# Decoder layer on one core: unnormalised attention turned behind the second product, normalised attention in the next slot, splits ahead of the root, PE's waits for stacks a slot ahead

## Chip, core and metric

One core of a Trainium2 chip. The metric is the device time of one execution in microseconds (us); lower is better. Engines are named as in the profile: PE (matmuls; PEld its weight loads), DVE, ACT, POOL, and SP, which here only issues DMAs.

## What is computed

A post-norm decoder layer without causal mask over 32 sequences of 128 tokens and width 128, in float32: self-attention, cross-attention to a context, and a feed-forward part with fake-quantised integers, each followed by a residual and a layer norm.

```python
x = _layernorm(x + attn(x, wq, wk, wv, bq, bk, bv, wo, bo))      # 16 heads of 8
x = _layernorm(x + xattn(ctx, x, ctx, Wk, Wq, Wv, Wo))           # 16 heads of 8, no bias
x = _layernorm(x + ffn(x, W1, b1, W2, b2))                       # per-tensor int8 grids, exact gelu
```

## The kernel before

**Tasks and slots.** The attention part is 64 tasks, each one sequence of self (S) or cross (C) attention; tasks come in pairs (two sequences), 32 pairs in the order S0 to S5, then C0, S6, C1, S7 and so on to C9, S15, then C10 to C15. `over_slots` runs `slot(k)` for k from -5 to 67 on every engine, so the order of all instructions is written out by hand, engine by engine, and engines meet only in semaphores. In slot k PE works on several tasks at once: the first scores of task k+2 (called b in the code), the second scores of k and k-1 (a, z), the product with v of k-1 (z), and the closing steps of k-2 (w), k-3 (x) and k-6 (v).

**Two passes of scores.** Keys and queries are split into float16 parts and laid out by DMA in "stacks" (`arena_h`), four heads side by side, so that a matmul with few rows gives a head's scores. The first pass (L1083) goes into two PSUM banks, 1024 columns per half task, and DVE takes the row maximum over 128 keys of each of 8 heads (`neg_max`, L850). The maximum is turned by PE (L1156), copied and scaled by ACT (L657) and sent by DMA into a row of the stack, so that the second pass (L1090) gives shifted scores, from which ACT makes the exponentials (L652 and L663). Both passes are interleaved in `scores(half)`; a half can start when DVE has finished the maximum of the half before (semaphore `max_done`, in the code `mx`) and ACT its exponentials (`ex`).

**Closing steps of a task.** `product(half)` (L1109) gives unnormalised attention and the sums; ACT copies it (L673), PE turns it in two pieces (L1167, semaphore `tu`), DVE takes the reciprocal of the sums (L860) and multiplies (L869), PE turns the result (L1199, `ta`), ACT copies it (`attT`, L680), PE multiplies with the output weights (L1191, `oo`), DVE adds the residual (L890), takes statistics (L829) and mean and variance (L833, semaphore `ag`), POOL makes the root (`var_eps` L528 and `rstd` L531), and DVE writes the new x (L841, `xn`).

**The way of a stack.** The projection of a pair (PE L1124, L1131, L1144) is copied by ACT (L619, L646, L690) to `q_full`, `k_full`, `cq_full`, `ck_full`. POOL splits it in two instructions (helper `split`, L364 and L366), and SP sends it with three DMAs (`fill`, L399) of 64 KB. For a pair whose first task has place p, POOL splits sq or ck in slot p-5 and sk or cq in slot p-4; SP fills in the order sq, sk or ck, cq in its slot p-4. PE needs both stacks in `scores(0)` of slot p-2, which is an even slot. POOL's work in a slot is in this order: the root of a task, the split of sk or cq, `x_bias` (L549), the context values (L560), the split of sq or ck. Within a queue everything waits for what stands before it.

**After the attention** come the feed-forward stages (from 275 us in the profile), which the change does not touch.

Of the kernel before, what the change touches and what calls it, by code (L numbers as in the profile page):

```python
# [25 lines left out]
NTERM = 3  # L26
# [136 lines left out]
def decoder_layer(nc, xT, xN, cT, cN, wq, wk, wv, bq, bk, bv, woT_u, bo, Wk, Wq, Wv, woT_x,  # L163
                  w1T, b1, w2T, b2, out):
    with ExitStack() as ctx:
# [303 lines left out]
        def _(pool):  # L469
# [54 lines left out]
            def slot(k):  # L524
                for v in outputs(k):

                    pool.wait_ge(ag, v.pos + 1)
                    pool.tensor_tensor(var_eps[v.par][:, :], mean_var[v.place][:, 1:2], eps_col[:, :], ALU.add).then_inc(ve, 1)  # L528
                    pool.wait_ge(ve, v.pos + 1)
                    need(pool, xn, v.pos - 3)  # L530
                    pool.tensor_tensor(rstd[v.place][:, :], var_eps[v.par][:, :], minus_half[:, :], ALU.pow).then_inc(rq, 1)  # L531
# [5 lines left out]
                if i is not None:  # L537

                    pool.wait_ge(txe, 2 * i + 2)
                    split(pool, "cq", cq_full[i % RING][:, :], i)  # L540
                i = S_FIRST.get(k + BIAS_AT)
# [63 lines left out]
        def _(act):  # L605
# [4 lines left out]
            def slot(k):  # L610
                a, z, w, v, nxt = task(k), task(k - 1), task(k - 2), task(k - 6), task(k + 1)
# [41 lines left out]
                if nxt is not None:  # L653
# [20 lines left out]
                if w is not None:  # L674

                    act.wait_ge(ta, w.pos + 1)
                    if v is not None and v.kind == "S":
                        act.wait_ge(tx, v.m + 1)
                    need(act, oo, w.pos)
                    act.copy(attT[:, :], ps_x[:, 0:S]).then_inc(tae, 1)  # L680
# [81 lines left out]
        def _(dve):  # L762
# [61 lines left out]
            def slot(k):  # L824
# [32 lines left out]
                if w is not None:  # L857
                    u = ps_t[:, 0:2 * S].rearrange("p (h c) -> p h c", c=16)
                    dve.wait_ge(tu, w.pos + 1)
                    dve.reciprocal(r_sum[:, :], u[:, :, E]).then_inc(rs, 1)  # L860
# [5 lines left out]
                if w is not None:  # L866
                    dve.wait_ge(rs, w.pos + 1)
                    need(dve, ta, w.pos)
                    dve.tensor_tensor(att[:, :, :], u[:, :, 0:E], r_sum[:, :].unsqueeze(2).broadcast_to([128, H, E]),  # L869
                                      ALU.mult).then_inc(an, 1)  # L870
                if k == 1:
                    folded_weights()
                if k == 2:
                    weight_top()
# [3 lines left out]
                if k == 2:  # L878
                    weight_scale()
                    own_step(dve.reciprocal(w_inv[:, :], w_scale[:, :]))  # L880
# [10 lines left out]
                if k <= LATE_STATS:  # L891
                    for t in outputs(k):
                        new_x(t)
                if late is not None:
                    mean_variance(late)
# [140 lines left out]
        def _(pe):  # L1036
# [19 lines left out]
            def slot(k):  # L1056
# [7 lines left out]
                def scores(half):  # L1064

                    s, s_half = (z, 1) if half == 0 else (a, 0)
                    if b is not None:
                        if half == 0 and b.half == 0:
                            for n in (b.q, b.k):
                                pe.wait_ge(s_stack[n][b.ring], landed(b.pair, RING, 16 * NTERM))  # L1070
                        need(pe, mx, 2 * b.pos + half)
                    if s is not None:
                        if s_half == 0:
                            pe.wait_ge(s_maxrow[s.par], 16 * (s.pos // 2 + 1))
                        need(pe, ex, 2 * s.pos + s_half)
                    for j in range(HQ):
                        for g in range(GROUPS_HALF):
# [9 lines left out]
                            if s is not None:  # L1087
# [4 lines left out]
                                if last:  # L1092
                                    ins.then_inc(p2, 1)

# [224 lines left out]
```

## Time and profile before

| | |
|---|---|
| median of 3 runs | 356.62 us (354.52 to 357.43) |
| profiled execution, its own time | 355.31 us |
| its span in the profile | 353.5 us |
| busy of the span: PE, DVE, ACT, POOL | 265.0, 314.0, 252.5, 187.0 us |
| attention part | to 274 us |
| granted TensorE clock, mean | 0.916 of full speed |

The profile is of one execution. Around its span lie 1.8 us that the profile does not see. Slots of the attention part can be told apart by DVE's `neg_max` instructions, two per slot.

### The profile page before, as it was taken

How to read it: one execution, taken by the hardware profiler on the slowest of the kernel's cores; microseconds unless marked ns; L12 is line 12 of the kernel's file. 1: busy time of each engine (PE TensorE's matmuls, PEld its weight loads, DVE VectorE, ACT ScalarE, POOL GpSimd, SP SyncE). 2: the span in 40 equal slices, each digit the busy share in tenths (PEclk: the TensorE clock that was granted, in tenths of full speed). 3: DMA queues.
4: the chain of work that ended last, by engine and by line, in shares of the span. 5: the costliest groups of instructions: out<-in, count | busy, mean ns of one | idle time of the engine just before them, and what ended most of it. 6: DMA issues, size and time to landing. Idle time of an engine off the chain costs nothing.

```text
span 353.5 us, 13237 instructions
## 1 busy us (share of the span) xinstructions
PE 265.0 (75%) x4897; PEld 171.0 (48%) x4899; DVE 314.0 (89%) x720; ACT 252.5 (71%) x502; POOL 187.0 (53%) x382
## 2 busy tenths in 40 slices
PE   3678887989989999999899988898883365102980
PEld 2446564656656666666665655555551122001660
DVE  5756799989999999999999999999889599997894
ACT  2135877988889888888888887887762599605855
POOL 6234869656675666657675667665222006400275
PEclk9999999999999999999999999999995578755797
DMA  1352323233332332323323242332000000000034
GB/s 52 89 159 69 99 80 88 63 108 90 97 107 74 107 104 84 101 84 102 106 83 107 79 124 84 96 94 71 5 3 0 0 0 0 0 0 3 1 90 149
DMA packets 48998, 25.19 MB, mean 71 GB/s; under 512 B 6440, under 2 KB 48808, under 8 KB 48936
## 3 DMA queue, kind: packets, MB, share of 16 engines
q1 hardware_dynamic: 46936, 23.76, 23.4%
q8 instruction: 41, 0.67, 0.8%
q10 hardware_dynamic: 2000, 0.59, 0.7%
q14 instruction: 21, 0.17, 0.2%
HBM read 9.39 MB, written 2.10 MB: 32 GB/s over the span
## 4 chain that ended last, share of the span: by engine, by line
DVE 32%; PE 30%; POOL 14%; issue 13%; DMA 4%; ACT 3%; SPq 2%; ACTq 0%; POOLq 0%; DVEq 0%; another core or an unknown queue 0%
DVE neg_max L850 14%; PE ps L1083 8%; PE ps L1109 7%; DVE h_ext L957 5%; DVE h_ext L958 5%; DMA arena_h<-parts_sk 4%; POOL rstd L531 3%; PE ps L1167 2%; PE ps L1156 2%; SPq L399 2%; PE ps L1124 2%; PE ps L1144 2%; PE ps L1131 2%; PE ps L1251 1%; POOL o_root L598 1%
## 5 line engine op out<-in xcount | busy, mean ns | idle before, releaser
L850 DVE TENSOR_REDUCE neg_max<-ps 128x8 f32<-128x1024 f32 x128 | 157.2, 1228 | 18.5 <-PE ps L1083 16.0
L652 ACT ACTIVATE probs<-ps 128x1024 f32<-128x1024 f32 x64 | 65.6, 1025 | 19.7 <-PE ps L1090 18.2
L1083 PE MATMUL ps<-arena_h 31*128 31x128 f16 x1024 | 52.8, 221 | 27.3 <-DVE neg_max L850 17.9
L663 ACT ACTIVATE probs<-ps 128x1024 f32<-128x1024 f32 x64 | 65.7, 1026 | 8.5 <-PE ps L1090 8.5
L1083 PEld LDWEIGHTS ps<-arena_h 31*128 31x128 f16 x1024 | 31.0, 94 | 59.9 <-DVE neg_max L850 35.6
L1090 PE MATMUL ps<-arena_h 32*128 32x128 f16 x1024 | 51.7, 219 | 0.6 <-ACT probs L652 0.5
L528 POOL TENSOR_TENSOR var_eps<-mean_var,eps_col 128x1 f32<-128x1 f32 x64 | 12.2, 191 | 73.4 <-DVE mean_var L833 73.4
L1109 PE MATMUL ps<-probs,arena_q 128*32 128x128 f32 x1024 | 42.1, 283 | 0.9 <-issue 0.9
L1109 PE MATMUL ps<-probs,arena_h 128*32 128x128 f32 x1024 | 41.6, 281 | 0.2 <-ACT probs L652 0.2
L531 POOL TENSOR_TENSOR rstd<-var_eps,minus_half 128x1 f32<-128x1 f32 x64 | 35.2, 550 | 5.0
L1090 PEld LDWEIGHTS ps<-arena_h 32*128 32x128 f16 x1024 | 29.6, 93 | 1.6 <-ACT probs L663 0.5
L1109 PEld LDWEIGHTS ps<-probs,arena_q 128*32 128x32 f32 x1024 | 24.5, 110 | 7.8 <-issue 1.4
L1109 PEld LDWEIGHTS ps<-probs,arena_h 128*32 128x32 f32 x1024 | 24.2, 109 | 6.9 <-ACT probs L652 0.4
L1167 PE MATMUL ps<-ident,u_sb 128*128 128x128 f32 x128 | 24.8, 276 | 0.0
L673 ACT COPY u_sb<-ps 128x256 f32<-128x256 f32 x64 | 23.6, 369 | 1.1 <-PE ps L1109 1.1
L957 DVE TENSOR_REDUCE h_ext<-arena_h 128x1 f32<-128x1024 f32 (+1 forms) x17 | 19.5, 1148 | 3.2 <-ACT arena_h L711 3.2
L680 ACT COPY attT<-ps 128x128 f32<-128x128 f32 x64 | 17.6, 276 | 5.6 <-PE ps L1199 5.5
L581 POOL TENSOR_TENSOR x_all<-x_all,b_wide 128x1024 f32<-128x1024 f32 x4 | 9.3, 2354 | 22.1 <-DVE x_int L952 22.1
L1199 PE MATMUL ps<-ident,att 128*128 128x128 f32 x64 | 18.0, 281 | 3.3 <-DVE att L869 3.2
L958 DVE TENSOR_REDUCE h_ext<-arena_h 128x1 f32<-128x1024 f32 (+1 forms) x17 | 19.5, 1146 | 0.0
L364 POOL TENSOR_TENSOR parts_sq<-q_full,zero_col 128x256 f16<-128x256 f32 x15 | 9.2, 612 | 18.2 <-ACT q_full L619 18.2
L711 ACT ACTIVATE arena_h<-ps,b_sb,quant 128x1024 f32<-128x1024 f32 (+1 forms) x17 | 18.6, 1194 | 0.3 <-remote 0.3
(155 smaller groups left out, 626.4 us busy)
## 6 DMA issues: line engine op xcount, KB each, us to landing
arena_h<-parts_sq SPq DMA_DIRECT2D x48, 64.0 KB, 2.0
arena_h<-parts_ck SPq DMA_DIRECT2D x48, 64.0 KB, 2.1
arena_h<-parts_cq SPq DMA_DIRECT2D x48, 64.0 KB, 2.0
arena_h<-parts_sk SPq DMA_DIRECT2D x45, 64.0 KB, 2.0
xT_in<-in_xT_dram SPq DMA_DIRECT2D x16, 128.0 KB, 2.6
xN_in<-in_xN_dram SPq DMA_DIRECT2D x16, 128.0 KB, 2.7
cT_in<-in_cT_dram SPq DMA_DIRECT2D x16, 128.0 KB, 2.4
cN_in<-in_cN_dram SPq DMA_DIRECT2D x16, 128.0 KB, 2.6
```

What stands on the lines that cost most here:

```text
L531: pool.tensor_tensor(rstd[v.place][:, :], var_eps[v.par][:, :], minus_half[:, :], ALU.pow).then_inc(rq, 1)
L652: act.activation(probs[1][:, :], ps_s2, ACT.Exp, scale=SCALE).then_inc(ex, 1)
L663: act.activation(probs[0][:, :], ps_s2, ACT.Exp, scale=SCALE).then_inc(ex, 1)
L673: act.copy(u_sb[:, :], ps_u[:, 0:2 * S]).then_inc(ue, 1)
L711: act.activation(hT[:, hc, tok], src, ACT.Gelu, bias=b1_sb[:, hc:hc + 1], scale=qs[0][:, OUT:OUT + 1]).then_inc(f_g, 1)
L850: dve.tensor_reduce(neg_max[b.par][:, HH * half:HH * half + HH], ps_s1.rearrange("p (h k) -> p h k", h=HH), AXX, ALU.max, negate=True).the ...
L957: dve.tensor_reduce(h_ext[:, 0, col:col + 1], h, AXX, ALU.max).then_inc(f_mx, 1)
L958: dve.tensor_reduce(h_ext[:, 1, col:col + 1], h, AXX, ALU.min, negate=True).then_inc(f_mx, 1)
L1083: ins = pe.matmul(ps_s1[:, at:at + S], q[r:r + MAX_AT, j, :], kk[r:r + MAX_AT, j, :], start=True, stop=True, skip_group_check=True)
L1090: ins = pe.matmul(ps_s2[:, at:at + S], kk[r:r + GROUP_ROWS, j, :], q[r:r + GROUP_ROWS, j, :], start=True, stop=True, skip_group_check=True)
L1109: last = pe.matmul(ps_u[32 * j:32 * j + 32, half * S:(half + 1) * S], heads_of[:, HQ * (GROUPS_HALF * half + g) + j, :], probs[half][:, (H ...
L1167: last = pe.transpose(ps_t[:, blk * S:(blk + 1) * S], u_sb[:, blk * S:(blk + 1) * S], ident[:, :])
```

## The change

The changes by engine:

The diff is in the order of the file: `roots`, then POOL, ACT and PE (whose helpers `scores` and `stacks` come first); DVE's part is left out.

- PE: the two transposes of `u_sb` stand behind `product(1)` and not behind `product(0)`. The transpose of `att` is made a slot later, behind `product(0)`, ahead of that of the maximum. The waits for a pair's stacks stand in a helper `stacks()` at the end of the slot before, ahead of the output product. In `scores` the wait for the maximum is written last.
- ACT: the copy `attT` stands in the next slot, between the scaled maximum and the copies of projections, and not at the slot's end.
- DVE: between the two maxima of a slot stand statistics, new x, and mean and variance; between the second and the next slot's first stand reciprocal, residual sum and multiplication.
- POOL: the splits of sk and cq stand ahead of the root, and the root is that of task k-4 and not of k-5 (helper `roots`).

```diff
+def roots(k):
+
+    if k <= LATE_STATS:
+        return [task(k - 4)] if task(k - 4) is not None else []
+    return [t for t in outputs(k) if t.pos > LATE_STATS - 4]
...
-                for v in outputs(k):
-
-                    pool.wait_ge(ag, v.pos + 1)
...
                 i = S_FIRST.get(k + FILL_AT)
                 if i:
                     pool.wait_ge(eqk, 2 * i + 2)
                     split(pool, "sk", k_full[:, :], i)
...
                     split(pool, "cq", cq_full[i % RING][:, :], i)
+                for v in roots(k):
+
+                    pool.wait_ge(ag, v.pos + 1)
...
+                if x is not None:
+                    act.wait_ge(ta, x.pos + 1)
+                    need(act, oo, x.pos)
+                    act.copy(attT[:, :], ps_x[:, 0:S]).then_inc(tae, 1)
                 if k >= LEAD_SLOTS:
                     evacuations()
...
-                    if b is not None:
-                        if half == 0 and b.half == 0:
-                            for n in (b.q, b.k):
-                                pe.wait_ge(s_stack[n][b.ring], landed(b.pair, RING, 16 * NTERM))
-                        need(pe, mx, 2 * b.pos + half)
                     if s is not None:
                         if s_half == 0:
                             pe.wait_ge(s_maxrow[s.par], 16 * (s.pos // 2 + 1))
                         need(pe, ex, 2 * s.pos + s_half)
+                    if b is not None:
+                        need(pe, mx, 2 * b.pos + half)
...
+                def stacks():
+
+                    t = task(k + 3)
+                    if t is not None and t.half == 0:
+                        for n in (t.q, t.k):
+                            pe.wait_ge(s_stack[n][t.ring], landed(t.pair, RING, 16 * NTERM))
...
                 scores(0)
                 product(0)
+                if x is not None:
+                    pe.wait_ge(an, x.pos + 1)
...
+                    pe.transpose(ps_x[:, 0:S], att[:, :, :].rearrange("p h e -> p (h e)"), ident[:, :]).then_inc(ta, 1)
...
                     pe.transpose(ps_x[0:H, S:2 * S], neg_max[nxt.par][:, :], ident[:, :]).then_inc(mt, 1)
+
+                if k >= LEAD_SLOTS:
+                    projections()
+
+                scores(1)
+                product(1)
...
                 if w is not None:
                     pe.wait_ge(ue, w.pos + 1)
                     need(pe, an, w.pos)
...
                     for blk in range(2):
                         last = pe.transpose(ps_t[:, blk * S:(blk + 1) * S], u_sb[:, blk * S:(blk + 1) * S], ident[:, :])
                     last.then_inc(tu, 1)
-
-                if k >= LEAD_SLOTS:
-                    projections()
-
-                scores(1)
-                product(1)
...
+                stacks()
                 if x is not None:
                     pe.wait_ge(tae, x.pos + 1)
...
                     pe.matmul(ps_o[:, 0:D], attT[:, :], (wo_self if x.kind == "S" else wo_cross)[:, :],
                               start=True, stop=True, skip_group_check=True).then_inc(oo, 1)
-                if w is not None:
-
-                    pe.wait_ge(an, w.pos + 1)
...
-                    pe.transpose(ps_x[:, 0:S], att[:, :, :].rearrange("p h e -> p (h e)"), ident[:, :]).then_inc(ta, 1)
```

PE at the end of slot 21, with the start of slot 22, before. In square brackets are the semaphores that PE waits for ahead of the instruction: the last-named is a wait of the instruction itself, those before it stand in wait instructions of their own, one or two in each.

```order
L1191 MATMUL ps<-wo_self,attT 128x128 [waits qk_full_out,y_done,attT_out]
L1199 MATMUL ps<-ident,att 128x128 [waits attT_out,cq_full_out,max_rows_out,att_done]
L1208 MATMUL ps<-ident,arena_q 128x128 [waits x_new_done]
L1083 MATMUL ps<-arena_h 128x128 [waits max_done,exp_done,stack_ck3_landed,stack_cq3_landed]
L1090 MATMUL ps<-arena_h 128x128
```

The same place now, from the turned u on:

```order
L1196 MATMUL ps<-ident,u_sb 128x128 [waits att_done,u_out]
L1196 MATMUL ps<-ident,u_sb 128x128
L1211 MATMUL ps<-wo_self,attT 128x128 [waits y_done,attT_out,qk_full_out,stack_ck3_landed,stack_cq3_landed]
L1218 MATMUL ps<-ident,arena_q 128x128 [waits attT_out,max_rows_out,x_new_done]
L1084 MATMUL ps<-arena_h 128x128 [waits max_done,exp_done]
L1091 MATMUL ps<-arena_h 128x128
```

The stacks' waits moved from the scores to the output product, and `max_done` still stands in a wait instruction ahead of the scores' first matmul. In the second half of slot 21, and in the first half of an odd slot, it stood on the matmul itself. Before:

```order
L1131 MATMUL ps<-xT_in1,wk_g 128x256 [waits qk_full_out,y_done]
L1083 MATMUL ps<-arena_h 128x128 [waits exp_done,max_row_landed1,max_done]
```

and now:

```order
L1162 MATMUL ps<-ident,att 128x128 [waits attT_out,cq_full_out,max_rows_out,att_done]
L1175 MATMUL ps<-ident,neg_max0 16x128 [waits attT_out,max_rows_out,cq_full_out,max_done,masks_ready]
L1139 MATMUL ps<-xT_in1,wk_g 128x256 [waits qk_full_out,y_done]
L1084 MATMUL ps<-arena_h 128x128 [waits max_done,exp_done,max_row_landed1]
```

So `max_done` went from the matmul to a wait instruction ahead of it. POOL from slot 24 (split of cq, pair C4) to slot 26 (split of sk, pair S10), before:

```order
L364 TENSOR_TENSOR parts_cq<-cq_full0,zero_col 128x256
L366 TENSOR_TENSOR parts_cq<-cq_full0,parts_cq 128x256
L528 TENSOR_TENSOR var_eps0<-mean_var0,eps_col 128x1
L531 TENSOR_TENSOR rstd0<-var_eps0,minus_half 128x1
L560 TENSOR_TENSOR arena_h<-cN_in0,zero_col 128x4x4x8 x2
L364 TENSOR_TENSOR parts_sq<-q_full,zero_col 128x256
L366 TENSOR_TENSOR parts_sq<-q_full,parts_sq 128x256
L528 TENSOR_TENSOR var_eps1<-mean_var1,eps_col 128x1
L531 TENSOR_TENSOR rstd1<-var_eps1,minus_half 128x1
L364 TENSOR_TENSOR parts_sk<-k_full,zero_col 128x256
L366 TENSOR_TENSOR parts_sk<-k_full,parts_sk 128x256
```

and now:

```order
L371 TENSOR_TENSOR parts_cq<-cq_full0,zero_col 128x256
L373 TENSOR_TENSOR parts_cq<-cq_full0,parts_cq 128x256
L544 TENSOR_TENSOR var_eps0<-mean_var0,eps_col 128x1
L547 TENSOR_TENSOR rstd0<-var_eps0,minus_half 128x1
L544 TENSOR_TENSOR var_eps1<-mean_var1,eps_col 128x1
L547 TENSOR_TENSOR rstd1<-var_eps1,minus_half 128x1
L567 TENSOR_TENSOR arena_h<-cN_in0,zero_col 128x4x4x8 x2
L371 TENSOR_TENSOR parts_sq<-q_full,zero_col 128x256
L373 TENSOR_TENSOR parts_sq<-q_full,parts_sq 128x256
L371 TENSOR_TENSOR parts_sk<-k_full,zero_col 128x256
L373 TENSOR_TENSOR parts_sk<-k_full,parts_sk 128x256
```

Two roots now stand together ahead of the context values and the split of sq; the split of sk follows that of sq at once. The second of the two (`mean_var1`) is that of slot 25's own mean and variance.

## Rows read from the trace of the kernel before

**Rows 1.** Busy time by engine in one stretch: from:to, length, PE, PEld, DVE, ACT, POOL.

```profile
62.00:206.00 144.00, 132.59 (x2906) 88.83 (x2894) 137.97 (x317) 123.55 (x272) 93.49 (x191) 1.00 0.33 94
```

**Rows 2.** The chain that ended last: start, length, what, from 125 us.

```profile
125.32 0.24 issue
...
129.03 0.04 issue
```

**Rows 3.** Timeline of DVE, end of slot 24 to the start of 26.

```profile
120.59 1.23 DVE L850 TENSOR_REDUCE neg_max<-ps 128x8 f32<-128x1024 f32 x1
...
122.32 1.23 DVE L850 TENSOR_REDUCE neg_max<-ps 128x8 f32<-128x1024 f32 x1
123.46 0.25 DVE L860 RECIPROCAL r_sum<-ps 128x16 f32<-128x16 f32 x1
123.63 0.23 DVE L829 BATCH_NORM_STATS2 stats<-y_sb 128x6 f32<-128x128 f32 x1
...
124.09 1.23 DVE L850 TENSOR_REDUCE neg_max<-ps 128x8 f32<-128x1024 f32 x1
125.23 0.28 DVE L890 TENSOR_TENSOR y_sb<-ps,x_bias 128x128 f32<-128x128 f32 x1
125.43 0.34 DVE L841 TENSOR_SCALAR x_all<-y_sb,mean_var,rstd 128x128 f32<-128x128 f32 x1
125.68 0.17 DVE L833 BATCH_NORM_AGGREGATE mean_var<-stats 128x2 f32<-128x6 f32 x1
126.01 1.23 DVE L850 TENSOR_REDUCE neg_max<-ps 128x8 f32<-128x1024 f32 x1 [0.15 <-PE ps L1083]
```

**Rows 4.** Timeline of DVE and PE at the two shared extremes.

```profile
273.94 0.17 DVE L943 TENSOR_REDUCE ext<-x_ext 128x2 f32<-128x18 f32 x1
...
274.17 0.37 PE L1224 MATMUL ps<-ident,ext 128*2 128x128 f32 x1 [3.54 <-DVE ext L943]
...
319.62 0.19 DVE L973 TENSOR_REDUCE ext<-h_ext 128x2 f32<-128x34 f32 x1
...
319.95 0.37 PE L1224 MATMUL ps<-ident,ext 128*2 128x128 f32 x1 [18.01 <-DVE ext L973]
```

**Rows 5.** Timeline of POOL, slots 25 and 26.

```profile
122.44 0.19 POOL L528 TENSOR_TENSOR var_eps<-mean_var,eps_col 128x1 f32<-128x1 f32 x1 [1.55 <-DVE mean_var L833]
...
123.22 0.76 POOL L560 TENSOR_TENSOR arena_h<-cN_in,zero_col 128x128 f32<-128x128 f32 x2
123.94 0.61 POOL L364 TENSOR_TENSOR parts_sq<-q_full,zero_col 128x256 f16<-128x256 f32 x1
...
126.72 0.61 POOL L364 TENSOR_TENSOR parts_sk<-k_full,zero_col 128x256 f16<-128x256 f32 x1
```

**Rows 6.** Timeline of SP at pair S10, and landings of all sk fills from 62 us.

```profile
125.37 2.38 SPq L399 DMA_DIRECT2D arena_h<-parts_sq  x3
128.11 1.92 SPq L399 DMA_DIRECT2D arena_h<-parts_sk  x3
...
DMA to landing us min/median/max: 1.9/2.1/3.5
```

**Rows 7.** First and last of 25 fills: chain and timeline at S6 and C15.

```profile
71.31 3.48 DMA arena_h<-parts_sk
...
72.53 1.23 DVE L850 TENSOR_REDUCE neg_max<-ps 128x8 f32<-128x1024 f32 x1
...
243.11 2.26 SPq L399 DMA_DIRECT2D arena_h<-parts_cq  x3
...
246.19 1.23 DVE L850 TENSOR_REDUCE neg_max<-ps 128x8 f32<-128x1024 f32 x1
```

**Rows 8.** Timeline of DVE and POOL at 66.5 us.

```profile
66.67 0.63 DVE L841 TENSOR_SCALAR arena_q<-y_sb,mean_var,rstd 128x128 f32<-128x128 f32 x1
...
66.55 0.67 POOL L366 TENSOR_TENSOR parts_sq<-q_full,parts_sq 128x256 f16<-128x256 f32 x1
```

**Rows 9.** Timeline of ACT in slot 25.

```profile
123.75 0.47 ACT L619 ACTIVATE k_full<-ps,bqk_sb 128x256 f32<-128x256 f32 x1 [0.22 <-PE ps L1131]
```

More of the change, by code:

```diff
@@ L540, in slot @@
                     split(pool, "cq", cq_full[i % RING][:, :], i)
+                for v in roots(k):
+                    pool.wait_ge(ag, v.pos + 1)
+                    pool.tensor_tensor(var_eps[v.par][:, :], mean_var[v.place][:, 1:2], eps_col[:, :], ALU.add).then_inc(ve, 1)
+                    pool.wait_ge(ve, v.pos + 1)
+                    need(pool, xn, v.pos - 3)
+                    pool.tensor_tensor(rstd[v.place][:, :], var_eps[v.par][:, :], minus_half[:, :], ALU.pow).then_inc(rq, 1)
                 i = S_FIRST.get(k + BIAS_AT)
@@ L673, in slot @@
                     act.copy(u_sb[:, :], ps_u[:, 0:2 * S]).then_inc(ue, 1)
-                if w is not None:
[L676 to L680, printed above, removed]
                 if k == 3:
@@ L865, in slot @@
                         new_x(t)
[L866 to L870, printed above, removed]
+                if k <= LATE_STATS:
+                    for t in outputs(k):
+                        new_x(t)
+                if late is not None:
+                    mean_variance(late)
                 if k == 1:
                     folded_weights()
-                if k == 2:
-                    weight_top()
+                if k == 3:
+                    weight_scale()
+                    own_step(dve.reciprocal(w_inv[:, :], w_scale[:, :]))
                 maximum(1)
@@ L877, in slot @@
                     weight_extremes()
-                if k == 2:
-                    weight_scale()
-                    own_step(dve.reciprocal(w_inv[:, :], w_scale[:, :]))
+                if w is not None:
+                    u = ps_t[:, 0:2 * S].rearrange("p (h c) -> p h c", c=16)
+                    dve.wait_ge(tu, w.pos + 1)
+                    dve.reciprocal(r_sum[:, :], u[:, :, E]).then_inc(rs, 1)
                 if x is not None:
@@ L890, in slot @@
                     dve.tensor_tensor(dst, own, residual, ALU.add).then_inc(yy, 1)
[L891 to L895, printed above, removed]
+                if w is not None:
+                    dve.wait_ge(rs, w.pos + 1)
+                    need(dve, ta, w.pos)
+                    dve.tensor_tensor(att[:, :, :], u[:, :, 0:E], r_sum[:, :].unsqueeze(2).broadcast_to([128, H, E]),
+                                      ALU.mult).then_inc(an, 1)
+                if k == 2:
+                    weight_top()
                 if k >= LATE_STATS and x is not None:
@@ L1148, in slot @@
                 product(0)
+                if x is not None:
+                    pe.wait_ge(an, x.pos + 1)
+                    need(pe, mte, tasks_to(k))
+                    need(pe, tae, x.pos)
+                    need(pe, txe, s_to(k - 7))
+                    pe.transpose(ps_x[:, 0:S], att[:, :, :].rearrange("p h e -> p (h e)"), ident[:, :]).then_inc(ta, 1)
+                    if x.pos == 0:
+                        pe.wait_ge(w_diag, 1)
+                        pe.matmul(ps_t[:, 3 * S:3 * S + 2], ones_2[:, :], w_top_diag[:, :], start=True, stop=True,
+                                  skip_group_check=True).then_inc(w_shared, 1)
                 if nxt is not None:
@@ L1192, in slot @@
                               start=True, stop=True, skip_group_check=True).then_inc(oo, 1)
[L1193 to L1195 removed]
+                if v is not None and v.kind == "S":
+                    pe.wait_ge(xn, v.pos + 1)
                     need(pe, mte, tasks_to(k + 1))
                     need(pe, tae, tasks_to(k - 3))
[L1198 to L1207 removed]
                     pe.transpose(ps_x[:, 2 * S:3 * S], x1_all[:, v.m, :], ident[:, :]).then_inc(tx, 1)
```

28 lines of the change are left out of this document (6 added, 22 removed).

## The prediction, as it was made

> **What bounds the kernel now.** I read, in this order, the busy times by stage, the chain that ended last, the timelines of DVE, POOL and SP over slots 24 to 28, and the rows where something is late. The stage from 62 to 206 us is DVE's: 137.97 busy of 144.00 us [rows 1]. The chain goes from `neg_max` to PE's scores and back, twice a slot. A half slot is 1.23 us of maximum and a gap in which PE makes the next half's scores: in slot 25 the first maximum ends at 123.55 and the second starts at 124.09 (gap 0.54); that one ends at 125.32 and slot 26's first starts at 126.01 (gap 0.69) [rows 3]. Ahead of odd slot 25 the gap is 0.50 (120.59 + 1.23 to 122.32) [rows 3]. The 0.19 more comes ahead of every even slot, where PE also waits for two stacks: the chain has 0.24 us of "issue" at 125.32 and 0.04 at 129.03 [rows 2]. DVE's small instructions fit in these gaps and start at distances of 0.15 to 0.25 us [rows 3].
>
> **A wait instruction that stands behind a late semaphore.** The built program puts `max_done`, in the even case, in the first of two wait instructions ahead of the matmul, in the odd case on the matmul itself; so two instructions are run after the maximum, for 0.19 us. A second pair of rows gives the price of one: L1224 starts 0.06 us after DVE's L943 where it waits for it itself (273.94 + 0.17 to 274.17), and 0.14 us after L973, for which a wait instruction stands ahead (319.62 + 0.19 to 319.95) [rows 4]. So 0.08 to 0.10 us each.
>
> **Part 1, order of the waits.** The change takes the stacks' waits out of the scores, but writes `max_done` last, and the built order then puts it in a wait instruction ahead of the matmul in all halves. Gap now: 0.50 + 0.08 = 0.58, I take 0.59 for each. A pair of slots has four gaps: before 0.69 + 0.55 + 0.50 + 0.54 = 2.28; now 4 x 0.59 = 2.36. The gap of 0.54 before the second half was PE's own work (a projection stands there), and the change takes one transpose of two from it; that gain goes under the 0.59. Over 27 pairs of slots: +2 us, between 0 (0.57) and +4 (0.61). The gain that one would read from the diff, 27 x 0.19 = 5 us, is given back three times over one half each.
>
> The Trainium skill says the same of waits ("Perfetto Trace Analysis", Identifying Dependency Chains): an instruction that waits for several engines may get EventSemaphore instructions ahead of it. It gives no price; by the rule alone the sum would have the stacks' waits cheaper by one place and nothing on the other halves. The sum above goes by rows 2 to 4.
>
> **Part 2, PE, ACT and DVE.** The turns of u and att only change places: PE loses 0.11 us between product(0) and scores(1) and gains it behind product(1), where it waits for DVE anyway. ACT's copy of `attT` goes where ACT idles 0.22 us for a projection [rows 9]: nothing, since the next exponentials wait for PE's scores; at worst 0.1 us a slot, if the copies reach past them. On DVE the gap within a slot now holds statistics, new x and mean: 0.16 + 0.25 + 0.2, the other reciprocal, residual and multiplication: 0.17 + 0.20 + 0.2 (distances in rows 3); both begin 0.09 us before the maximum ends, so both fit in 0.59. Tail and early slots: the same work, 0, within 1 us.
>
> **Part 3, the splits, which decides.** Before, POOL in slot 25 waited for mean and variance from the end of slot 24 (var_eps at 122.44), then context values at 123.22, split of sq at 123.94; the sk split starts at 126.72 and ends at 128.08 [rows 5]. Now the root in slot 25 is that of slot 25's own statistics. DVE's mean ends at about the first maximum's start + 1.74 = 124.06. So var_eps starts at 124.14, +0.78 root, +0.72 values: the split of sq starts at 125.64, 1.7 us later than before. The split of sk follows at once and is ready at 128.36, only 0.3 later, for it no longer has a root ahead. But SP is one queue: sq's three DMAs start at 127.08 (before 125.37), take 1.92 as those of sk did, and sk's start at 129.00 (before 128.11), 0.9 us later [rows 6]. The same sum for cross pairs (the ck split is held, x_bias takes the place of the values) gives cq 0.83 later.
>
> What margin is there? Before, the third DMA of sk for S10 starts near 129.4 and lands 1.9 later, 131.3, and PE needs it when the second maximum of slot 27 ends, at 132.5: 1.2 us. Now 0.9 is lost and 0.12 won by longer slots: 0.4. And the wait stands earlier. Behind it on PE are the output product and the turn of x1; DVE's residual sum waits for that product, and the next maximum stands behind the sum. From a landing to that maximum I count 0.14 (a wait instruction and start) + 0.49 (product) + 0.05 + 0.20 + 0.20 = 1.1 us, against a normal 0.59 after the maximum's end; so a fill is late when its margin is under 0.5. Undisturbed fills then cost 0.1 us each.
>
> Most aren't undisturbed: sk's DMAs land in 1.9 to 3.5 us, median 2.1 [rows 6]. The same subtraction over the 25 fills from S6 (71.31 + 3.48 = 74.79 against a maximum's end of 72.53 + 1.23 = 73.76: -1.03) to C15 (all three issued by 243.11 + 2.26 = 245.4, the last landed at 246.7, against 246.19 + 1.23 = 247.42: +0.7) [rows 7] gives a mean of 0.57. Moved by 0.75 and needed 0.49 earlier, that lacks 0.67 us a fill, 17 us in all if each paid by itself. It doesn't: a fill's way spans 2.5 slots, so when one pair stalls, the next has that much more time. Taking each stall off the next lack, in order, leaves 11 us; 1.2 of it is paid before (S6, S8). So +10 us. Bounds: +4 (the fills are 0.5 us less late than I count), +20 (two fills back to back issue and land slower, as S6 did).
>
> The Trainium skill's advice for DMAs ("DMA: Bandwidth & Descriptors", Rules for kernel authors) is to issue early and to wait late. The change does the reverse in both; rows 5 to 7 put its price here.
>
> **Part 4, new x beside a split.** New x took 0.63 in place of 0.34 us at 66.67, and ended 0.08 after the POOL split at 66.55 to 67.22 [rows 8]: it reads and writes SBUF only, and waits for POOL. In the new place it stands 1.30 after a slot's start; in even slots POOL then has the first instruction of a split, to about 1.66, and if DVE gets in between the two, it ends at 1.74, ahead of the maximum at 1.82: 0. If it doesn't, 0.6 us for each of 27 slots, 16 us. I take 0 to 4, +1, since the two instructions of a split are 0.08 us apart. The skill ("GPSIMD Engine Reference", Key points) names this sharing of the SBUF interfaces; it has no time for it.
>
> **Sum.** 355.3 (own time of the profiled execution) + 2 + 10 + 1 = 368. The median of the runs shown is 1.3 above that execution, well within the error of the 10. An effect under 1% (3.6 us) can't be told from none.
>
> **Rivals.**
> 1. *The stacks are in time, only the waits' order counts.* For it: on a calm fill the margin of 0.4 misses 0.5 by 0.1, and the longer slots give more. Against: the spread of landings. Time: 355.3 + 2 = 357. Chance 0.13.
> 2. *Faster: the wait instructions cost nothing once they are ahead.* The price at the scores comes only from two of them in a row, a single one is hidden under PE's weight load, and the stacks are in time; this decides from the point where less than 0.04 us of the 0.08 is seen. Then all gaps are 0.50: 27 x (2.28 - 2.00) = 7.6, and the stalls of S6 and S8 go: 347 to 349. For it: sk's own split is no longer behind a root, and the diff gathers all waits away from the scores. Against: rows 4 show a single one at 0.08, and SP's queue order. Chance 0.09.
> 3. *Contention decides*: new x waits for both parts of a split in each even slot, stalls of the stacks are partly covered by it: 355.3 + 2 + 16 + 4 = 377. Chance 0.15.
> 4. My forecast, about 368 (360 to 374): 0.63.
>
> **How the numbers follow.** Slower by over 1%: 0.63 + 0.15 = 0.78; within 1%: 0.13; faster: 0.09. The range reaches from rival 1 to rival 3: 355 to 379.
>
> **What would show it.** PE's L1084 waiting for DMAs of sk and cq, or, since the wait moved, PE's output product L1211 doing so, in more than 10 places and over 8 us in total; POOL's sq split starting 3.3 us after a slot's first maximum instead of 1.6; calm gaps between maxima of 0.58 to 0.60 in all four places; no "issue" of 0.24. Wrong if the gaps are 0.50 (then a single wait instruction is free), or if fills land more than 1 us before use. Rival 3 shows in new x rows over 0.5 us that end with a POOL split.

## The result, and the profile after

The changed kernel takes 373.9 us (median of 4 runs, 370.2 to 376.5), the kernel before beside it 355.8 us (4 runs): 1.050 times as long, interval 1.044 to 1.056. Its profiled execution took 373.43 us, with a span of 371.7. The span before was 353.5, so 18.2 us are to be explained.

**Where the 18.2 us lie.** I cut both traces at DVE's maxima (L850 before, L854 now):

| stretch | before | after | difference |
|---|---|---|---|
| start of the span to slot 9's first maximum | 63.6 | 67.5 | +4.0 |
| from there to slot 61's second maximum | 189.7 | 205.0 | +15.2 |
| from there to the end | 100.2 | 99.2 | -1.0 |

The middle stretch holds 53 slots, and the maxima themselves take the same in both (129.8 and 129.5 us). The rest of it are the gaps ahead of them, in sum:

| gap ahead of | before | after |
|---|---|---|
| an even slot's first maximum | 19.4 | 28.0 |
| its second | 14.1 | 17.3 |
| an odd slot's first | 13.6 | 15.9 |
| its second | 14.6 | 15.9 |

Busy times by engine, for the stretch of [rows 1]: DVE is busy for 129.05 us instead of 137.97, so it waits more. The granted clock of TensorE, third from the end, is 0.99 instead of 1.00.

```profile
62.00:206.00 144.00, 128.46 (x2671) 84.52 (x2670) 129.05 (x292) 116.66 (x251) 87.09 (x179) 0.99 0.31 88
```

DVE's timeline of the calm slot 25, which answers to [rows 3]:

```profile
129.74 0.27 DVE L896 TENSOR_TENSOR att<-ps,r_sum 128x128 f32<-128x128 f32 x1
130.10 1.23 DVE L854 TENSOR_REDUCE neg_max<-ps 128x8 f32<-128x1024 f32 x1
131.24 0.28 DVE L833 BATCH_NORM_STATS2 stats<-y_sb 128x6 f32<-128x128 f32 x1
131.44 0.33 DVE L845 TENSOR_SCALAR x_all<-y_sb,mean_var,rstd 128x128 f32<-128x128 f32 x1
131.69 0.18 DVE L837 BATCH_NORM_AGGREGATE mean_var<-stats 128x2 f32<-128x6 f32 x1
131.91 1.22 DVE L854 TENSOR_REDUCE neg_max<-ps 128x8 f32<-128x1024 f32 x1
...
133.73 1.23 DVE L854 TENSOR_REDUCE neg_max<-ps 128x8 f32<-128x1024 f32 x1
```

Here the gaps are 131.91 - 131.33 = 0.58 and 133.73 - 133.13 = 0.60, where they were 0.54 and 0.69. DVE's small instructions end 0.04 to 0.09 us ahead of the next maximum (131.69 + 0.18 against 131.91), so they fit, as costed.

POOL's timeline for the same slot, and the start of the next; it answers to [rows 5]:

```profile
131.94 0.19 POOL L544 TENSOR_TENSOR var_eps<-mean_var,eps_col 128x1 f32<-128x1 f32 x1 [2.64 <-DVE mean_var L837]
132.21 0.55 POOL L547 TENSOR_TENSOR rstd<-var_eps,minus_half 128x1 f32<-128x1 f32 x1
132.72 0.76 POOL L567 TENSOR_TENSOR arena_h<-cN_in,zero_col 128x128 f32<-128x128 f32 x2
133.44 0.61 POOL L371 TENSOR_TENSOR parts_sq<-q_full,zero_col 128x256 f16<-128x256 f32 x1
134.13 0.67 POOL L373 TENSOR_TENSOR parts_sq<-q_full,parts_sq 128x256 f16<-128x256 f32 x1
134.76 0.61 POOL L371 TENSOR_TENSOR parts_sk<-k_full,zero_col 128x256 f16<-128x256 f32 x1
135.45 0.67 POOL L373 TENSOR_TENSOR parts_sk<-k_full,parts_sk 128x256 f16<-128x256 f32 x1
```

The root waits 2.64 us for a mean that ends in the middle of the slot, and only then come values, split of sq, split of sk. The split of sq starts 3.34 us after the slot's first maximum (133.44 - 130.10). SP then sends what POOL has left behind. The rows answer to [rows 6]. The last one is for the five DMAs that SP issued from 135.4 to 138.1 us; the longest of them, 2.9, is the third of sk, issued at 138.09:

```profile
134.87 1.82 SPq L406 DMA_DIRECT2D arena_h<-parts_sq  x3
136.74 1.95 SPq L406 DMA_DIRECT2D arena_h<-parts_sk  x3
...
DMA to landing us min/median/max: 1.9/2.4/2.9
```

So the stack is there at 141.0, while the last maximum that needs nothing of it ends at 140.39. DVE and PE at that place, the end of slot 27:

```profile
139.17 1.22 DVE L854 TENSOR_REDUCE neg_max<-ps 128x8 f32<-128x1024 f32 x1
140.31 0.25 DVE L882 RECIPROCAL r_sum<-ps 128x16 f32<-128x16 f32 x1
141.60 0.29 DVE L892 TENSOR_TENSOR y_sb<-ps,arena_q 128x128 f32<-128x128 f32 x1 [1.04 <-PE ps L1211]
...
142.01 1.21 DVE L854 TENSOR_REDUCE neg_max<-ps 128x8 f32<-128x1024 f32 x1
```

```profile
141.10 0.46 PE L1211 MATMUL ps<-wo_cross,attT 128*128 128x128 f32 x2 [1.03 <-issue]
```

The gap is 1.62 instead of 0.59 us. Note what the last row gives as the cause: "issue". The wait for the stack is in a wait instruction of its own ahead of the matmul, and the profile doesn't always trace such a wait to its DMA. The list of waits of the whole kernel after therefore has them under three names:

```profile
POOL var_eps L544 <- DVE mean_var L837: 95.8, 48, 3.7
DVE y_sb L892 <- PE ps L1211: 14.5, 13, 2.4
PEld ps L1211 <- issue: 13.4, 10, 2.8
...
PEld ps L1211 <- DMA arena_h<-parts_cq: 4.4, 6, 1.8
```

The second row is the one that counts, for DVE sets the pace: 13 times the residual sum waited for an output product, 14.5 us in all; before, it did so once, for 1.0 us. The first row was 73.4 us in 62 places before.

The page's chain, which had "DVE 32%; PE 30%; POOL 14%" of the span before, now runs through POOL:

```profile
POOL 36%; issue 33%; DVE 17%; PE 9%; ACT 2%; DMA 1%; POOLq 0%; ACTq 0%; DVEq 0%; another core or an unknown queue 0%
```

Read such an "issue" with the timeline beside it. A piece of it on this chain goes from 136.90 to 139.16; the first row of the list of waits says what POOL waited for there: the mean of the next slot. It is a wait for DVE, and no cost of issuing.

**The early part**, slots 2 to 8. PE's product of 16 matmuls, after:

```profile
34.84 1.08 PE L1117 MATMUL ps<-probs,arena_q 128*32 128x128 f32 x16 [0.69 <-issue]
37.57 1.08 PE L1117 MATMUL ps<-probs,arena_q 128*32 128x128 f32 x16
39.68 0.64 PE L1117 MATMUL ps<-probs,arena_q 128*32 128x128 f32 x16 [0.22 <-issue]
```

and before:

```profile
30.44 1.08 PE L1109 MATMUL ps<-probs,arena_q 128*32 128x128 f32 x16
33.82 0.65 PE L1109 MATMUL ps<-probs,arena_q 128*32 128x128 f32 x16 [0.90 <-issue]
```

The same 16 matmuls took 1.08 us until 38.6 us after, and until 31.5 before. The step lies where the trace's first record of the granted clock begins, at 38.7 us after and at 31.5 before, with 1.00 (2.4 GHz) in both; the 1.00 that the profile prints for earlier times only says that there is no record. In slot 8 the record falls to 0.50 (1.2 GHz) from 62.6 to 66.0 us after, and the 16 matmuls take 1.08 us again; before, it stays at 1.00. So up to 38.7 us the matmuls ran at the pace of the lower clock. The lines are the product in slot 8 and the stretch around it, as from:to, length, PE, granted clock, share and GB/s of the DMAs, first after and then before:

```profile
62.58 1.08 PE L1117 MATMUL ps<-probs,arena_q 128*32 128x128 f32 x16
62.00:66.00 4.00, 4.00 (x63) 0.58 0.37 108
```

```profile
62.00:66.00 4.00, 3.89 (x90) 1.00 0.29 85
```

Ahead of this fall PE waited: it was busy for 1.42 of the 4 us from 58 to 62, since the stacks of S5 landed at 61.7 instead of 59.5. Slot 2's gaps were 2.34 and 2.27 us where they had been 1.17 and 1.80, and slot 8's 2.97 and 1.81 instead of 2.44 and 0.56. The changed kernel is 2.35 us behind at slot 3's first maximum (40.09 against 37.74), 2.65 at slot 8's and 4.0 at slot 9's; so nearly all of the 4.0 us arises in the two stretches in which its matmuls take the time of the lower clock and those of the kernel before don't.

In `a_order` and `a_root5` the profiled execution was a disturbed one with a lower granted clock, so of these two profiles only gaps and waits are read, and of the four runs of `a_order` only one, 365.5 us, was undisturbed (the others took 373.3 to 379.5).

### The profile page after: what moved, and what is told of

Same layout as the page of the kernel before. It is cut to its first block, busy times and chain, and to the rows that moved or that the text cites. A ratio compares the mean times of both kernels' runs of the same rounds, so it can differ in the third digit from the quotient of the medians.

```text
span 371.7 us, 13270 instructions
## 1 busy us (share of the span) xinstructions
PE 276.9 (75%) x4897; PEld 177.0 (48%) x4899; DVE 315.7 (85%) x720; ACT 257.1 (69%) x502; POOL 185.4 (50%) x382
## 4 chain that ended last, share of the span: by engine, by line
POOL 36%; issue 33%; DVE 17%; PE 9%; ACT 2%; DMA 1%; POOLq 0%; ACTq 0%; DVEq 0%; another core or an unknown queue 0%
POOL rstd L547 7%; DVE h_ext L961 5%; DVE h_ext L962 4%; POOL var_eps L544 3%; POOL arena_h L567 3%; POOL parts_ck L373 3%; POOL x_bias L556 3%; POOL parts_cq L371 3%; POOL parts_ck L371 2%; POOL parts_cq L373 2%; POOL parts_sq L373 2%; POOL parts_sq L371 2%; POOL parts_sk L371 2%; DVE neg_max L854 2%; PE ps L1084 1%
## 5 line engine op out<-in xcount | busy, mean ns | idle before, releaser
L854 DVE TENSOR_REDUCE neg_max<-ps 128x8 f32<-128x1024 f32 x128 | 156.4, 1222 | 21.4 <-PE ps L1084 16.0
L659 ACT ACTIVATE probs<-ps 128x1024 f32<-128x1024 f32 x64 | 65.5, 1024 | 30.1 <-PE ps L1091 29.0
L674 ACT ACTIVATE probs<-ps 128x1024 f32<-128x1024 f32 x64 | 65.5, 1024 | 9.1 <-PE ps L1091 7.0
L1084 PE MATMUL ps<-arena_h 31*128 31x128 f16 x1024 | 54.1, 224 | 19.2 <-DVE neg_max L854 11.6
L1084 PEld LDWEIGHTS ps<-arena_h 31*128 31x128 f16 x1024 | 33.7, 95 | 52.3 <-issue 31.8
L1091 PE MATMUL ps<-arena_h 32*128 32x128 f16 x1024 | 52.8, 222 | 0.6 <-ACT probs L659 0.6
L1117 PE MATMUL ps<-probs,arena_q 128*32 128x128 f32 x1024 | 43.6, 291 | 0.9 <-issue 0.9
L1117 PEld LDWEIGHTS ps<-probs,arena_q 128*32 128x32 f32 x1024 | 25.4, 114 | 8.2 <-issue 2.1
L1196 PE MATMUL ps<-ident,u_sb 128*128 128x128 f32 x128 | 28.2, 302 | 0.0
L1162 PE MATMUL ps<-ident,att 128*128 128x128 f32 x64 | 21.6, 338 | 4.2 <-DVE att L896 4.2
L1211 PE MATMUL ps<-wo_cross,attT 128*128 128x128 f32 x64 | 14.2, 305 | 8.2 <-issue 7.3
L668 ACT COPY attT<-ps 128x128 f32<-128x128 f32 x64 | 15.3, 239 | 5.8 <-PE ps L1162 5.8
L1196 PEld LDWEIGHTS ps<-ident,u_sb 128*128 128x128 f32 x128 | 13.2, 143 | 12.3 <-issue 12.3
```

Source lines behind the costliest of these rows:

```text
L659: act.activation(probs[1][:, :], ps_s2, ACT.Exp, scale=SCALE).then_inc(ex, 1)
L674: act.activation(probs[0][:, :], ps_s2, ACT.Exp, scale=SCALE).then_inc(ex, 1)
L854: dve.tensor_reduce(neg_max[b.par][:, HH * half:HH * half + HH], ps_s1.rearrange("p (h k) -> p h k", h=HH), AXX, ALU.max, negate=True).the ...
L1084: ins = pe.matmul(ps_s1[:, at:at + S], q[r:r + MAX_AT, j, :], kk[r:r + MAX_AT, j, :], start=True, stop=True, skip_group_check=True)
L1091: ins = pe.matmul(ps_s2[:, at:at + S], kk[r:r + GROUP_ROWS, j, :], q[r:r + GROUP_ROWS, j, :], start=True, stop=True, skip_group_check=True)
L1117: last = pe.matmul(ps_u[32 * j:32 * j + 32, half * S:(half + 1) * S], heads_of[:, HQ * (GROUPS_HALF * half + g) + j, :], probs[half][:, (H ...
```

## The experiments

Names with a_ are the changed kernel with one or more parts taken back, those with b_ the kernel before with one part added. Ratios are to the kernel before in the same session (medians 354.1, 354.1 and 353.7 us). "Stage" is the middle stretch of the first table: 189.7 us before, 205.0 after.

### `a_roots`: the root at the slot's start again

```diff
             def slot(k):
+                for v in outputs(k):
+                    pool.wait_ge(ag, v.pos + 1)
...
-                for v in roots(k):
-                    pool.wait_ge(ag, v.pos + 1)
```

> The changed kernel, but POOL makes the root where it made it before: at the start of its slot, of task k-5, ahead of all splits. Its mean and variance are then half a slot old, so POOL need not wait. Theory 'POOL's wait in mid slot makes sq and ck late': the split of sq starts 1.6 us earlier against the slot or more, the stalls of over 1 us in even slots mostly go, calm gaps stay 0.59: 373.9 - 12 = 360 to 364. Rival 'the stacks are late because PE waits for them ahead of the output product': stays within 3 us of 374.

Measured: 356.9 us, ratio 1.009 (1.005 to 1.013); stage 193.0; calm gaps 0.59 in all four places. Gaps that exceed the calm one by more than 0.1 us, called stalls from here on, are four, 2.4 us above it in sum; the changed kernel has 17, with 14.4 us. POOL and SP, slots 25 and 26:

```profile
121.30 0.19 POOL L535 TENSOR_TENSOR var_eps<-mean_var,eps_col 128x1 f32<-128x1 f32 x1 [0.25 <-DVE mean_var L837]
...
122.79 0.61 POOL L371 TENSOR_TENSOR parts_sq<-q_full,zero_col 128x256 f16<-128x256 f32 x1
...
125.65 0.61 POOL L371 TENSOR_TENSOR parts_sk<-k_full,zero_col 128x256 f16<-128x256 f32 x1
```

```profile
124.23 2.73 SPq L406 DMA_DIRECT2D arena_h<-parts_sq  x3
127.04 1.85 SPq L406 DMA_DIRECT2D arena_h<-parts_sk  x3
```

With slot 25's first maximum at 121.21, the split of sq starts 1.58 us after it, as before, and the first DMA of sk 5.8 us after it instead of 6.6. Of the 5.0% that the change costs, 4.1 go with this one part. The time is below the 360 to 364 us that I expected, since the early part came back too (slot 9 at 63.3 us, with the full clock from 29.5 us on).

### `a_root5`: the root behind the split, but an older task's

```diff
-                for v in roots(k):
+                for v in outputs(k):
```

> The changed kernel, but the root that stands behind the splits of sk and cq is that of task k-5, as before the change, whose mean and variance are half a slot old; nothing else differs. Theory 'what makes the fills late is that POOL waits for the middle of DVE's slot': the loss of the late fills goes as in a_roots, 355 to 360. Rival 'it is the place behind the split that matters': stays at 370 or more.

Measured: 362.4 us, ratio 1.021 (1.015 to 1.027). The stalls ahead of even slots are gone (1.1 us in two places, calm gap 0.59), and no output product waits for a DMA. So it is whose root stands there that makes the stacks late, not that a split stands ahead of it. The place has a price of its own, and that I had too low: in even slots the gap ahead of the second maximum is 0.81 us, since new x now waits for a root that begins behind a split.

```profile
POOL var_eps L544 <- DVE mean_var L837: 45.5, 36, 3.7
...
DVE arena_q L845 <- POOL rstd L547: 7.5, 14, 2.3
```

### `a_stacks`: the stacks' waits behind the output product

```diff
-                stacks()
                 if x is not None:
                     pe.wait_ge(tae, x.pos + 1)
...
                     pe.matmul(ps_o[:, 0:D], attT[:, :], ...).then_inc(oo, 1)
+                stacks()
```

> The changed kernel, but stacks() stands behind the output product and not ahead of it, so that no instruction that DVE waits for stands behind the stacks' waits. Theory: a late fill then costs 0.5 us less in each of some 12 places: 366 to 371. Rival 'only the place of that wait is at fault': 357 to 361, since before the change the fills were in time for the scores.

Measured: 368.7 us, ratio 1.042 (1.034 to 1.049); stalls 10.2 us in 14 places instead of 14.4 in 17; stage 200.7. DVE's residual sum no longer waits for a late stack, and the stalls are 4.3 us less. The interval overlaps that of the changed kernel, but the stage, 4.3 us shorter, says the same as the stalls. It is the smaller part.

### `a_order` and `b_last`: the order of the waits

`a_order` writes the maximum's wait first again in the changed kernel; `b_last` writes it last in the kernel before, and changes nothing else.

```diff
-                        need(pe, mx, 2 * b.pos + half)
                     if s is not None:
...
                         need(pe, ex, 2 * s.pos + s_half)
+                    if b is not None:
+                        need(pe, mx, 2 * b.pos + half)
```

> The changed kernel, but in scores() the wait for the maximum is written first again, so that the build puts it on the matmul itself and the exponentials' wait ahead of it. If a wait instruction behind the late semaphore costs 0.09 us, calm gaps between maxima fall from 0.59 to 0.50. Theory 'late stacks decide': slots get 0.36 us a pair shorter, but the fills' way from POOL's root to landing stays as long, so the stalls grow by nearly as much: time 367 to 373, 0 to 6 us below the changed kernel. Rival 'the order of the waits is the whole loss': back to 352 to 358.

> The kernel before with one edit: in scores() the wait for the maximum is written last, so that the build puts it in a wait instruction ahead of the matmul in every half; the stacks' waits stay in the scores. Theory (0.09 us for a wait instruction behind the late semaphore): gaps 0.69, 0.59, 0.59, 0.59 in place of 0.69, 0.55, 0.50, 0.54, that is 0.18 us in each of 27 pairs of slots, +4 to +5 us, 1.3% slower than before. Rival 'the calm gap of 0.59 in the changed kernel comes from DVE's new order': gaps stay, same as before.

Measured, `b_last`: 357.6 us, ratio 1.011 (1.006 to 1.015), stage 192.5. All four gaps are 0.59, while I had expected 0.69 to stay ahead of even slots. DVE's maxima in it, at a distance of 1.82 us throughout:

```profile
119.87 1.23 DVE L850 TENSOR_REDUCE neg_max<-ps 128x8 f32<-128x1024 f32 x1
121.68 1.22 DVE L850 TENSOR_REDUCE neg_max<-ps 128x8 f32<-128x1024 f32 x1
123.50 1.23 DVE L850 TENSOR_REDUCE neg_max<-ps 128x8 f32<-128x1024 f32 x1
```

The built program tells why. PE's first scores of an even slot, in the kernel before and in `b_last`:

```
L1083 MATMUL ps<-arena_h 128x128 [waits max_done,exp_done,stack_sk0_landed,stack_sq0_landed]
L1084 MATMUL ps<-arena_h 128x128 [waits exp_done,max_done,stack_sk0_landed,stack_sq0_landed]
```

The maximum's wait has moved back by one place; a gap of 0.59 fits one instruction run after it, where 0.69 fitted two. Stalls are 1.9 us in six places instead of 1.2 in two, so some 0.7 of the stage's 2.8 us are late stacks again.

Measured, `a_order`: 365.5 us, ratio 1.032, from a single run. It speaks against the rival (352 to 358) and lies just below my 367 to 373; how much the order is worth here it can't tell. The calm gaps fell to 0.50 in all four places, as costed. Its profile shows more waits for late stacks than the changed kernel's (22.3 us in 18 places instead of 14.5 in 13), as expected of shorter slots; but in that execution the granted clock was at 0.50 in six stretches between 90 and 265 us, so that this isn't shown. The order's worth is read from `b_last`, in which the stacks mostly come in time.

### `b_waits`: what one would hope from the diff

The kernel before, with the stacks' waits out of `scores` and ahead of the turn of `att`, and the maximum's wait on the matmul.

```diff
-                        if half == 0 and b.half == 0:
-                            for n in (b.q, b.k):
-                                pe.wait_ge(s_stack[n][b.ring], landed(b.pair, RING, 16 * NTERM))
...
+                stacks()
                 if w is not None:
```

> The kernel before with one edit: the stacks' waits stand ahead of the transpose of att at the end of the slot before, and the maximum's wait stays written first, so it is on the matmul itself in every half. Theory (0.09 us for each wait instruction behind the maximum's semaphore, fills with a mean margin of 0.57 us): gaps ahead of even slots fall from 0.69 to 0.50, 27 x 0.19 = 5 us, less what shorter slots take from the fills' margin: 350 to 353, 3 to 6 us faster than before. Rival 'the two wait instructions cost nothing, the 0.19 has another cause': same as before.

Measured: 354.0 us, ratio 1.000 (0.996 to 1.004). The gap of 0.69 is gone:

```profile
118.89 1.23 DVE L850 TENSOR_REDUCE neg_max<-ps 128x8 f32<-128x1024 f32 x1
120.61 1.23 DVE L850 TENSOR_REDUCE neg_max<-ps 128x8 f32<-128x1024 f32 x1
122.38 1.23 DVE L850 TENSOR_REDUCE neg_max<-ps 128x8 f32<-128x1024 f32 x1
124.11 1.23 DVE L850 TENSOR_REDUCE neg_max<-ps 128x8 f32<-128x1024 f32 x1
```

Gaps of 0.49, 0.54 and 0.50. Yet the time is the same. Eleven gaps ahead of even slots were stalls, 4.9 us in all, where the kernel before had 1.2 us in two; the stage is 188.3 us, 1.4 shorter, and the median doesn't show that. The gain of 0.19 us in every second slot is real and was mostly given back.

### `b_end`: the root behind all splits, to get the stacks out earlier

`b_waits` with POOL's root (of task k-5) moved to the end of the slot's work.

```diff
-                for v in outputs(k):
...
                     split(pool, "ck", ck_full[:, :], i)
+                for v in outputs(k):
```

> The kernel before with the stacks' waits ahead of the transpose of att (as b_waits) and with POOL's root (still of task k-5) behind all splits of its slot. b_waits had calm gaps of 0.50 in even slots but 3.9 us of stalls for late fills. Theory: without a root ahead the splits come 0.8 us earlier or more, the stalls go to under 1 us: 3 to 5 us faster than before, 349 to 351 where before has 354. Rival 'the fills are late by SP and the DMAs themselves': the stalls stay near 4 us, same as before.

Measured: 367.8 us, ratio 1.040 (1.036 to 1.045). My theory fell. The stacks of the 25 pairs from S6 on did come earlier, now 1.3 to 3.5 us ahead of need (in the kernel before 1.2 ahead to 1.0 late), but the split of ck waits for ACT, and the root stands behind it. POOL and DVE in slots 24 and 25:

```profile
119.44 0.61 POOL L364 TENSOR_TENSOR parts_ck<-ck_full,zero_col 128x256 f16<-128x256 f32 x1 [3.76 <-ACT ck_full L646]
...
121.03 0.55 POOL L571 TENSOR_TENSOR rstd<-var_eps,minus_half 128x1 f32<-128x1 f32 x1
```

```profile
121.61 0.62 DVE L841 TENSOR_SCALAR arena_q<-y_sb,mean_var,rstd 128x128 f32<-128x128 f32 x1 [0.86 <-POOL rstd L571]
...
122.25 1.19 DVE L850 TENSOR_REDUCE neg_max<-ps 128x8 f32<-128x1024 f32 x1
```

DVE waited 0.86 us for the root, then ran beside a split for 0.62 instead of 0.34, and the maximum started 1.69 us after the last one's end (119.34 + 1.22 to 122.25).

### `a_all` and its three neighbours

The turns and DVE's order stay as the change has them; the maximum's wait is first, the stacks' waits stand behind the output product, the root is at the slot's start (the three edits shown above together).

> The changed kernel's new places of the turns on PE, ACT and DVE, with the other three parts undone or mended: the maximum's wait written first, the stacks' waits behind the output product, POOL's root of task k-5 at the start of its slot. Theory: calm gaps of 0.50 in all four halves, few stalls, since in this place POOL never waits for DVE: 348 to 352 where before has 354. Rival 'turning u behind the second product costs by itself': 355 or more.

Measured: 350.1 us, ratio 0.990 (0.985 to 0.995), stage 186.8. It is 1% faster than the kernel before, and faster than the changed one. So the places of the turns cost nothing that a run can tell, and if anything help; no run has them alone.

`a_all_end` is `a_all` with the root behind all splits.

> As a_all, but the root of task k-5 stands behind all of POOL's splits. Theory: the splits are earlier still, the last stalls of late fills go: 347 to 351, as a_all or up to 2 us below it. Rival 'the root then comes too late for new x in the middle of the slot': DVE waits ahead of new x, 356 or more.

Measured: 424.2 us, ratio 1.201 (1.195 to 1.208). The same loop as in `b_end`, with DVE's new x half a slot earlier and so with less slack for a late root. The granted clock fell to 0.50 again and again in this kernel (0.827 in the mean, against 0.916 in `b_end`), and no run tells what of the 20% is due to that:

```profile
POOL parts_ck L371 <- ACT ck_full L653: 77.3, 16, 7.4
DVE arena_q L845 <- POOL rstd L578: 36.8, 14, 3.0
```

`a_two` is `a_all` with the stacks' waits ahead of the output product, as the change has them; `a_best` has them ahead of it for self pairs and behind it for cross pairs.

```diff
+                if v is None or v.kind == "C":
+                    stacks()
...
+                if v is not None and v.kind == "S":
+                    stacks()
```

> a_all, but with the stacks' waits ahead of the output product, where the change has them. So only POOL's root and the order of the waits are as before. Theory (fills need a margin of 0.5 us here, and a_all has several cross pairs under that, but even slots with a cross task to close no longer have the 0.69): 350 to 354, within 2 us of a_all. Rival 'the place of the stacks' waits costs 5 us as it did beside late fills': 355 or more.

> a_all, where the stacks' waits of self pairs (margins of 1.5 to 3.8 us in a_all) stand ahead of the output product and those of cross pairs behind it. In a_all the gap ahead of every second even slot was still 0.70, since no x1 transpose follows there and the waits fall on the scores again. Theory: those gaps fall to 0.50, 11 to 13 of 0.19 us, 2 us below a_all: 346 to 350, 1.5% faster than before. Rival 'calm gaps shorten but fills stall more': as a_all.

Measured: `a_two` 351.7 us, ratio 0.993 (0.990 to 0.997), stage 188.2; `a_best` 350.1 us, ratio 0.986 (0.982 to 0.991), stage 186.0. Among the three the intervals overlap: where the stacks come in time, the place of their waits makes at most some 2 us. In `a_best` gaps ahead of even slots fell to 0.50 as meant, 15.6 us in sum instead of the 17.6 of `a_all`. But ahead of even slots' second maxima they grew from 14.0 to 15.6, and there new x takes 0.57 us beside a split in twelve slots, where in `a_all` it takes 0.54 to 0.57 in five. The 2 us under `a_all` that I expected are not there.

## Why the prediction was right, and where its size was off

- **The splits decide: right.** Late stacks were to cost +10 us (bounds 4 to 20). Ahead of even slots' first maxima there are twelve stalls, 12.6 us above the calm gap, against two with 1.2 before: +11.4. `a_roots` and `a_root5` show that the cause is the root of the slot's own statistics. The details hold too: the split 3.34 us after the first maximum (forecast 3.3); S10's stack late by 0.6 us; from landing to next maximum 142.01 - 141.01 = 1.0 (counted 1.1). After each stalled self pair but one (S14) the next cross pair had 0.6 to 1.5 us to spare, which is the alternation that brought 17 down to 11.
- **The waits' order: right.** Forecast +2 with all gaps at 0.59. The calm gaps are 0.59, 0.59, 0.59 and 0.59, and in `b_last` the order alone costs 3.7 us by the ratio (2.1 to 5.4) and 2.8 us in the stage. So it is in the upper half of my bounds; in the changed kernel itself the calm gaps give 27 x (2.36 - 2.28) = 2.2.
- **New x beside a split: right in size.** Forecast +1. Of 55 instructions between 62 and 275 us, 15 took over 0.36 us, together some 2 us more than the others. One of them, and the POOL split beside it:

```profile
127.62 0.69 DVE L845 TENSOR_SCALAR arena_q<-y_sb,mean_var,rstd 128x128 f32<-128x128 f32 x1
```

```profile
127.56 0.67 POOL L373 TENSOR_TENSOR parts_cq<-cq_full,parts_cq 128x256 f16<-128x256 f32 x1
```

  DVE ends at 128.31, 0.08 after POOL, as in [rows 8]. Most of it is under the next gap: only the three longest (0.69, 0.71 and 0.73, in slots 24, 32 and 50) are followed by a stall, 0.7 us in sum. Rival 3 (16 us of it) is out.
- **Two small terms that the sum lacks.** The other two stalls ahead of a second maximum are neither late stacks nor new x. In slot 16 (0.8 us) PE's projection started at 96.06, when the load of its input `xT_in` had landed at 95.97; SP had issued it at 92.20, behind the late DMAs of a pair. In slot 54 (0.4 us) the granted clock was 0.50, from 243.5 to 246.9. The middle stretch as a whole: 11.4 late stacks, 2.2 order, 0.7 new x, 0.8 and 0.4 these two, 0.3 less for the maxima, together 15.2.
- **Tail: right.** 0 forecast, -1.0 measured.
- **Early slots: this term was off.** "Tail and early slots: the same work, 0, within 1 us" failed for the early slots, which cost 4.0 us. It is the same work, but at the pace of the lower clock for longer, and the prediction had no term for the clock. Together with the 2 us by which the middle stretch exceeds its 13, it is why the time is 373.9 and not 368, still within the range. The profiles of the experiments bear the clock out. In each kernel whose record begins by 32.2 us and has no fall before slot 9, slot 9's first maximum starts at 62.9 to 64.4 us: so the kernel before, the four with the root of k-5 at the slot's start (`a_roots`, `a_all`, `a_two`, `a_best`), all three b_ kernels, and `a_order` too, whose root waits in mid slot. `a_stacks` (up at 32.6, a fall at 59.9) has it at 65.5, the changed kernel at 67.5, `a_root5` (up at 38.7, a fall at 59.2) at 69.2. What makes the clock rise late stays open: POOL's queue alone doesn't, for `a_order` is up at 29.4. Each of these is one execution.
- **The rivals.** The one that was slower through contention and the one with stacks in time are answered above. The faster one (a single wait instruction is free) is refuted by `b_last`. But its number, 347 to 349, is close to the 350 of `a_best`, with its gaps ahead of even slots at 0.50. The sign that I gave against myself, fills that land more than 1 us before use, did come for some pairs (C13 by 2.6 us), though not on average (0.22 us over the 25 fills, 0.57 before).

The Trainium skill's advice on DMAs ("DMA: Bandwidth & Descriptors", Rules for kernel authors), to issue early and to wait late, agrees with `a_roots` (4.1% for issuing the pair's DMAs 0.8 to 1.8 us earlier) and, more weakly, with `a_stacks`. `b_end` is its limit: the DMAs came earlier, and the kernel got 4% slower.

## What to carry to other kernels

On an in-order queue ask of each instruction not what it costs but how late its inputs are, and what stands behind it: the root takes 0.78 us wherever it stands, and its place in POOL's queue was worth from 1% (`a_root5` against `a_roots`) to 21% (`a_all_end` against `a_all`, the lower clock included). A stall removed at one wait is only a gain if the transfers behind it had that much slack; count the margin of each fill before and after, and undo one part at a time, since here one edit cost 4%, and behind it were another that cost 1% and a rest that is 1% faster than before. Write the wait that comes last so that it ends up on the instruction itself, and look in the built order whether it did.

## What was not expected

- With the maximum's wait written one place later, the gap ahead of even slots fell from 0.69 to 0.59 us, although the same four waits stand there (`b_last`), and in odd slots it rose from 0.50 to 0.59: what counts is how many instructions run after the late semaphore, 0.09 us for each.
- The same 16 matmuls changed from 1.08 to 0.64 us at 31.5 us in one kernel and at 38.6 in the other, and the windows of the profile print a granted clock of 1.00 for 20 to 40 us in both. They count a stretch without a record as 1.00; where the first record begins (31.5 and 38.7 us), the matmuls get faster. So a printed 1.00 at the start of a trace is to be checked against the time of a known instruction.
- New x takes 0.37 to 0.73 us where it meets POOL's split, instead of 0.33. The reverse, a POOL split slowed by it, is not to be seen: 0.67 with and without.
